# A transformer block with a mixture of experts on one core: the down product repacked to 128 rows, and the order around it

## What is computed

```python
xn = layernorm(x)                                  # (8, 256, 256)
q, k, v = xn @ Wq + bq, xn @ Wk + bk, xn @ Wv + bv # 16 heads of 16
q, k = rope(q), rope(k)
attn = softmax(causal(q @ k.T / 4)) @ v @ Wo + bo
scores = softmax(xn @ gate_w.T)                    # 64 experts, top 6 per token
routed = sum over the 6: w * (silu(g) * u) @ w_down[e].T   # g, u = xn @ w_gate_up[e].T, 176 wide each
shared = (silu(sg) * su) @ ws_down.T               # 2 shared experts of 176 (352 wide in all)
out = x + attn + routed + shared
```

## Time and profile before

| | us |
|---|---|
| three executions | 728.43, 731.99, 732.77 (median 731.99) |
| the profiled execution, its own time | 725.61 |
| its span, first to last instruction | 723.8 |
| busy in the span: PE, DVE, POOL, ACT | 674.7, 497.2, 396.6, 326.6 |
| mean granted TensorE clock | 0.981 of full speed |

### The profile page before, as it was taken

One profiled execution on the slowest core, in us unless ns is written; L12 is line 12 of the kernel. 1 busy time (PEld: TensorE's weight loads), 2 busy tenths in 40 slices (PEclk: granted clock), 3 DMA queues, 4 the chain that ended last, 5 costly groups with the idle time before them and its releaser, 6 DMA issues.

```text
span 723.8 us, 19510 instructions
## 1 busy us (share of the span) xinstructions
PE 674.7 (93%) x5200; PEld 434.2 (60%) x5202; DVE 497.2 (69%) x1184; ACT 326.6 (45%) x849; POOL 396.6 (55%) x383
## 2 busy tenths in 40 slices
PE   6899999989999999999999999999778998999996
PEld 3755677664555555555555555555456776677764
DVE  5498899856666666667666666656377779777751
ACT  2432322224444444444444444444446566656552
POOL 2000000227787777777787776763776776677520
PEclk9599999999999999999999999999989999999998
DMA  8500000037676766767676763342122312231310
GB/s 282 185 1 1 1 0 1 22 112 233 191 211 195 224 211 214 224 211 214 211 224 191 248 210 98 98 96 58 59 66 73 100 55 67 88 98 57 96 59 30
DMA packets 54288, 90.75 MB, mean 125 GB/s; under 512 B 8694, under 2 KB 32438, under 8 KB 54246
## 3 DMA queue, kind: packets, MB, share of 16 engines
q1 hardware_dynamic: 23494, 43.11, 19.9%
q0 software_dynamic: 10752, 29.37, 14.4%
q10 hardware_dynamic: 20000, 17.73, 7.3%
HBM read 69.21 MB, written 20.97 MB: 125 GB/s over the span
## 4 chain that ended last, share of the span: by engine, by line
PE 61%; DVE 9%; POOL 8%; DMA 7%; issue 6%; ACT 3%; DVEq 2%; SPq 2%; ACTq 1%; POOLq 0%
PE pair L1023 20%; PE pair L1058 10%; PE pair L933 6%; POOL wqkv_sb L436 5%; DMA lower<-wdn 5%; PE pair L1009 4%; PE bank L1032 3%; PE pair L1042 3%; PE bank L996 3%; DMA wqkv_sb<-y_rows,slot_i 3%; PE bank L1134 2%; DVE negm L829 2%; DVE space L806 2%; POOL space L432 2%; PE bank L1081 1%
## 5 line engine op out<-in xcount | busy, mean ns | idle before, releaser
L380 POOL DMA_INDIRECT lower<-xn_rows,idx_all x128 | 136.9, 1069 | 228.4 <-DVE idx_all L752 135.5
L1023 PE MATMUL pair<-space,work 128*64 (+1 forms) x768 | 166.0, 463 | 7.9 <-DMA lower<-wdn 3.3
L1058 PE MATMUL pair<-lower,work 88*64 x512 | 121.6, 379 | 1.3 <-ACT work L537 1.0
L1023 PEld LDWEIGHTS pair<-space,work 128*64 128x64 f32 x768 | 66.9, 136 | 80.3 <-issue 56.5
L522 ACT ACTIVATE work<-pair 128x176 f32<-128x176 f32 x160 | 51.5, 322 | 117.4 <-PE pair L1023 59.9
L1058 PEld LDWEIGHTS pair<-lower,work 88*64 88x64 f32 x512 | 69.6, 137 | 48.1 <-issue 11.2
L762 DVE TENSOR_TENSOR work<-work,pair 128x176 f32<-128x176 f32 x160 | 53.1, 333 | 60.5 <-ACT work L522 60.0
L812 DVE COPY space<-lower 88x512 f32 x64 | 78.8, 1231 | 22.2 <-issue 21.8
L1023 PE MATMUL pair<-wqkv_sb,work 128*64 128x352 f32 x256 | 89.4, 472 | 0.0
L529 ACT ACTIVATE lower<-pair 128x256 f32<-128x256 f32 x128 | 49.3, 385 | 77.7 <-PE pair L1058 77.7
L557 ACT ACTIVATE pT<-pair 128x768 f32<-128x768 f32 x64 | 52.0, 812 | 58.9 <-PE pair L1121 56.2
(11 more groups left out here) (171 smaller groups left out, 1346.9 us busy)
## 6 DMA issues: line engine op xcount, KB each, us to landing
space<-wgu SPq DMA_DIRECT2D x66, 352.0 KB
y_rows<-lower ACTq DMA_DIRECT2D x128, 128.0 KB
lower<-wdn SPq DMA_DIRECT2D x66, 176.0 KB
x_all<-x SPq DMA_DIRECT2D x4, 512.0 KB, 7.7
xn_rows<-qk_all SPq DMA_DIRECT2D x16, 128.0 KB, 2.0
lower<-xn_rows,idx_all POOLq DMA_INDIRECT x128
out<-x_all SPq DMA_DIRECT2D x8, 256.0 KB, 2.5
wqkv_sb<-wqkv SPq DMA_DIRECT2D x1, 768.0 KB, 12.5
```

The source lines that it names most:

```text
L380: po.indirect_dma_start(xg[:, r % XB, :], None, xn_rows[:, :], bass.IndirectOffsetOnAxis(idx_all[:, r:r + 1], 0)).then_inc(xg_in[r % XB], 16)
L1023: last = pe.matmul(pair[u % 2][strip, 0:2 * F], xgT[u][:, c, strip], n, start=c == 0, stop=c == EC - 1, skip_group_check=True)
L1058: last = pe.matmul(pair[u % 2][strip, 512:512 + E], hT[:, u % 2, c, strip], n, start=c == 0, stop=c == 1, skip_group_check=True)
```

## The change

**The down product.** The hidden features are laid out as 128 + 48 in place of 88 + 88. `hid` and `hT` hold two tiles in three blocks of 128: block 0 is tile 0's first 128 features, block 2 tile 1's, and block 1 the last 48 of tile 0 on rows 0 to 47 and the last 48 of tile 1 on rows 64 to 111. So two tiles take 3 transposes (`h_transpose` once a turn), one copy of 384 columns on ACT, and `down` for two tiles is 4 matmuls of 128 rows and then 4 of 48 rows, each of these in its own quarter of the array. The 48-row part of strip 0 reads `first_rest`, a new copy on DVE of 256 columns per tile (L849), because it must lie on the rows of its tile. The second product of `hidden` is two instructions (128 and 48 columns). `down` of both tiles waits for both copies of its turn (`rest_own`).

**Weights.** An expert is loaded by 5 DMAs in place of 2, the last 48 rows twice. POOL clears the unused rows of the ring in two pieces (`zeros_ok`).

**Registers.** PE's table `tile_s` holds the ring slot itself. PE no longer waits for weights (DVE's copy does). PE loads its registers between the 128-row and the 48-row matmuls. DVE loads two entries per tile, `own` and `first`, in place of one.

**Shared experts.** They run two tiles a turn, as the routed ones do, with 3 down matmuls of 128 rows for two steps (of one token tile, both experts) in place of 4 of 88. `LIST_AT` lists one token tile per turn.

**Attention.** The first nine scores alternate between `pair[0]` and `pair[1]`; the first two fills come before the last down product; `combine` comes before `normalise` in DVE's slot.

```diff
-LIST_AT = [3 * (t - LISTED_FIRST) // 2 - 1 for t in range(NT)]
+LIST_AT = [2 * (t - LISTED_FIRST) - (1 if t < 6 else 3) for t in range(NT)]
...
+                sp.dma_start(wdn_sb[0:FP, s, 0], dn[:, 0:E]).then_inc(w_loaded[s % 2], 16)
+                sp.dma_start(wdn_sb[FP:P, s, 0], dn[0:P - FP, E:2 * E]).then_inc(w_loaded[s % 2], 16)
+                sp.dma_start(wdn_sb[0:REST, s, 1], dn[P - FP:FP, E:2 * E]).then_inc(w_loaded[s % 2], 16)
+                sp.dma_start(wdn_sb[HALF:HALF + REST, s, 1], rest[P - FP:FP, E:2 * E]).then_inc(w_loaded[s % 2], 16)
...
             def hidden(i, u):
...
+                if k == 0:
+                    last = dve.tensor_tensor(hid[:, 0:F], sg[:, 0], up, ALU.mult)
+                else:
+                    dve.tensor_tensor(hid[:, 2 * P:3 * P], sg[:, 1, 0:P], up[:, 0:P], ALU.mult)
+                    last = dve.tensor_tensor(hid[:, P + HALF:P + HALF + REST], sg[:, 1, P:F], up[:, P:F], ALU.mult)
...
             def load_own(i, u):
                 dve.reg_load(own_reg[u], tile_e[0:1, 1, bass.ds(i, 1)])
+                dve.reg_load(first_reg[u], tile_e[0:1, 0, bass.ds(i, 1)])
...
+                e = dve.snap(first_reg[u], min_val=0, max_val=XT - 1) & (P - 1)
+                rows = slice(u % 2 * HALF, u % 2 * HALF + REST)
+                dve.tensor_copy(first_rest[rows], wdn_sb[rows, bass.ds((e + FIRST) % WB, 1), 1]
+                                .rearrange("p o n -> p (o n)")).then_inc(rest_own, 1)
...
-                wait_weights(pe, e)
...
+                pe.wait_ge(hT_ok, i + 2)
+                pe.wait_ge(rest_own, i - SHARED_TILES + 2)
...
+                for k in range(2):
+                    rows = slice(k * HALF, k * HALF + REST)
+                    for g, n in enumerate((first_rest[rows], own_dn[k][rows, 1])):
+                        strip = slice(g * GRAIN, (g + 1) * GRAIN)
+                        last = pe.matmul(pair[k][strip, 512:512 + E], h[rows, 1, strip], n, start=False, stop=True,
+                                         skip_group_check=True)
...
+        def scores_at(m):
+            return pair[m % 2 if m < AHEAD else 0][:]
```

More of the change, by code:

```diff
@@ L1027, in h_transpose @@
             def h_transpose(i, u):
[L1028 to L1034 removed]
+                o = bank[2 + u // 2]
+                pe.wait_ge(hid_ok, i + 2)
@@ L1064, in _ @@
[L1064 to L1070 removed]
+                for c, w in enumerate((wdn_sb[:, FIRST, 0], wdn_sb[:, FIRST, 1], wdn_sb[:, FIRST + 1, 0])):
+                    last = pe.matmul(pair[t % 2][:, 512:512 + E], hT[:, u // 2, c], w, start=c == 0, stop=c == 2)
```

230 lines of the change are left out of this document (136 added, 94 removed).

## The result

The changed kernel takes 776.93 us (median of six executions, 771.39 to 780.66); the kernel before, run beside it on the same chip, takes 732.34 us (728.43 to 734.2). The ratio is 1.061, with a 95% interval of 1.056 to 1.066: slower. The forecast was 729 us, and 776.93 lies outside its range. The profiled execution took 777.52 us with a span of 775.7 us and a mean granted clock of 0.944, where before it was 725.61, 723.8 and 0.981.

The account below looks back on a forecast made before the run. PE's work per turn was taken as the bound, DVE having 0.8 us of slack. Shared experts -5.5, weights +1, routed stage +6.7 and attention -5 gave -2.8 us, so 729 us on the median, range 715 to 743.

Parts of the forecast that it names:

- PE's turn, 4.83 us: Routed stage: PE's own work per turn falls from 5.28 to 4.83 us, with the 48-row products at 0.43.
- the guess of 0.1: PE's routed turn: 0.1 us added for changing the split of the array.
- The third rival: Routed down part: quarters run two by two, so it stays at 1.73 us; kernel 721 us; chance 0.12.
- DVE's turn, 5.50 us: Routed stage: DVE's sequencer becomes the bound at 5.40 to 5.64 us a turn, 5.50 taken; stage +6.7 us.
- My price of 0.41 us for a second load: DVE's routed turn: the added register load per tile costs 0.30 us plus 0.11 for its address step.
- The second rival: DVE's routed turn 6.0 us: loads at median or more (+0.48), POOL's blocking no longer hidden (+0.15); 760 us; chance 0.21.
- the third case: Slower case on whose side the prediction put the 600 ns load floor (turn 6.6 us, kernel some 64 us slower).
- Shared experts, -5.5: Shared stage: PE's shorter turns give -8.8 us, DVE's lateness +2, eight register loads +1.3; bounds -9 and 0.
- weights, +1: Between shared and routed stages: three more DMA issues per expert delay the first weights by 1 us; bounds 0 and +4.
- the 4.5: Shared stage: DVE's work per turn, 4.5 us, against PE's 3.99 and 0.35 for the listing.
- Attention, -5: Attention: two score buffers -2.2 us and `combine` ahead of `normalise` -2.8, sum -5; bounds -8.7 and +4.
- The ramp's -2.2: Start of attention: two score buffers shorten the distance between maxima from 2.45 to 1.7 us in three slots, -2.2 us.

Follow-up runs that it names:

- p0: The kernel before without POOL's rotary step, its biases and the output bias, gathers kept: 726.3 us, ratio to before 0.988 to 0.995.
- p3: Changed kernel without POOL's tensor work, one register load per tile on DVE, hidden copy first on ACT: 728.6 us, ratio to before 0.993 to 1.000.
- p1: Changed kernel without POOL's rotary step, its biases and the output bias, gathers kept: 751.6 us, ratio to before 1.020 to 1.034.
- p2: Changed kernel without POOL's tensor work and with one register load per tile on DVE: 742.2 us, ratio to before 1.009 to 1.020.
- a2: Changed kernel with one register load per tile on DVE in place of two: 771.6 us, ratio to before 1.036 to 1.057.
- a1: Changed kernel with `combine` put back behind `normalise`, `halves` and `residual` in DVE's attention slot: 765.4 us, ratio to before 1.035 to 1.051.
- a4: Changed kernel with down weights laid out by the host, two DMAs per expert in place of five: 784.5 us, ratio to before 1.048 to 1.066.
- c5: c4 with five DMAs per expert in place of two: 735.8 us, ratio to before 1.002 to 1.008.
- c4: c3 with the hidden copy ahead of the transposed x copies on ACT: 734.6 us, ratio to before 1.002 to 1.008.
- c3: Changed kernel with sums behind `normalise`, PE's late wait for the 48-row copies, one DVE load per tile, two DMAs per expert: 728.0 us, ratio 0.995 to 0.999.
- w1: Changed kernel with PE's wait for the 48-row copies (`rest_own`) moved behind the 128-row down products: 765.8 us, ratio to before 1.041 to 1.052.
- b1: The kernel before with `combine` ahead of `normalise`, `halves` and `residual` in DVE's attention slot: 744.9 us, ratio to before 1.013 to 1.024.
- a5: Changed kernel with PE's two register loads moved behind the 48-row products: 774.8 us, ratio to before 1.055 to 1.067.

## Why the prediction was wrong

**What bounds before.** PE's work per turn, with DVE 0.8 us in reserve. p0 fits: 4.2 us are all that POOL's tensor work cost there.

**PE's turn, 4.83 us.** Right as PE's own chain: 4.89 us in p3. Four 128-row pairs took 0.86 as forecast; the tails 0.59, up to the start of the transposes, for 0.43 and the guess of 0.1. The third rival is refuted, the quarters run together; the "pace of the array" by which attention's four products were read had no row behind it, so this was the first measurement. But in the changed kernel PE's turn is only reached when nothing waits, and a wait of 0.3 us ahead of the down part lengthens the part itself, to 1.97 us. The prediction had no such term.

**DVE's turn, 5.50 us: the step that failed.** It is the sentence "Contention does not come on top: the second down copy takes 1.26 us in the mean where the first took 0.42, blocked while POOL works, but the sequencer runs on behind it." With POOL at work the turn is 6.02 us, without its tensor work 5.66 (p1). The blocking is 0.37 us x 63 = 23 us of the changed kernel's stage, and 18.8 of the 37.4 that the change added. The sum without contention came near, 5.50 against 5.66, in part by luck: it has one value where p1's turns alternate between 5.2 and 6.0, and ACT's hidden copy is missing from it. The reasoning held before the change, when a blocked copy had its reserve to run out in. It failed because the down copies, the added one last, are what PE waits for, and because two copies stand behind each other on one engine, so a blocked one delays the next. That the sequencer goes on is of no use when the copy itself is waited for.

**The rest of the 37.4.** Without POOL's tensor work the changed kernel is still 0.30 us a turn over the old one (5.66 against 5.36), by DVE's sequencer and ACT's hidden copy in turn. p1, p2 and p3 take the covers off one by one: 5.66, 5.55, 5.33. My price of 0.41 us for a second load was too low for DVE itself: the two down copies of a turn start 1.67 us apart in the median of p1 (forecast 1.47) and 1.12 apart in p2, so the load costs DVE 0.55. But it was far too high for what it is worth to the kernel: 0.11 a turn in p2, where PE then waited for ACT, and 0.02 in the profile of a2. ACT I had called "still under PE's turn"; it was over it, since `hT_copy` stood behind `xgT_copy` and half of the up part.

**The second rival** named 6.0 us a turn, two loads at their median and blocking by POOL. The turn was 6.02, but by luck in the size: the place and the blocking were right, its price of 0.15 less than half of what it measured (0.37, or 0.30 more than in the old kernel), and the loads wrong (0.31 us in the median). Its sign, down copies that start more than 1.6 us apart, was met: 1.70 in the median of the changed kernel. Its 760 us missed through the other terms. The Trainium skill's floor of about 600 ns for a `tensor_load` (DMA: Bandwidth & Descriptors, section "Latency and other measured facts"), which the prediction tied to "the third case" and which points to this one, was not seen: the medians are 308 and 311 ns.

**Shared experts, -5.5, and weights, +1.** Right in size: from the first shared to the first routed up product it is 4.0 us less, for -4.5. The turn of 4.33 us, seen seven times, is the forecast's 3.99 and 0.35 for the listing, so there DVE needed less than the 4.5; in the three late turns it was late by more than the 0.16 forecast. The eight loads ahead of the first product were put at +1.3, and PE's wait there is 3.14 us. That the routed stage starts only 2.4 earlier is because the shared one began 1.6 later in this execution (0.3 in a1, with the same code ahead of it). Two DMAs per expert bring the start forward by 1.5 us in a4 and 1.7 between c5 and c4, near the +1. Of the 5.2 us by which c3 starts earlier (153.6), a2, a4 and w1 show 1.8, 1.5 and 1.0 alone.

**Attention, -5: wrong in sign.** `combine` ahead of `normalise` was put at -2.8, with a bound of +4 for rows that come late "in each of the sequences". It costs 15.1 us in a1 and 18.4 in b1. I had priced the waits that go, not what stands behind the instruction that would now wait: `normalise`, and behind it PE's projection, and behind that a clock that falls once per sequence (0.91 in attention; 0.98 in the profile before from 505 to 720 us, 0.93 in p0 and c3, where the sums also come last). The ramp's -2.2 did not show.

**The clock.** No term was given to it. In the routed stage it fell after waits of PE of 1.47, 1.89, 1.45 and 1.49 us, and added to each of them. After four others of that size (1.41 at 270.23, 1.81 at 339.89 and at 410.13, 1.55 at 486.21) it didn't, and what makes the difference stays open.

## What to carry to other kernels

Reserve that an engine has is reserve of a place in the order, not of a percentage: before you put a copy on an engine, ask who waits for that copy, and what the longest blocked copy of its kind takes (2.06 us here for a mean of 0.57 and a shortest of 0.28). Put a wait for late data behind the work that does not need it; w1 got 13.6 us in the stage by moving one line. And where four engines stand within 0.3 us of each other, an edit must be tried with the others around it: the same swap on ACT made p2 13.7 us faster, the changed kernel no faster and c3 6.6 us slower.

## What was not expected of the hardware

An idle PE can pay twice. In the changed kernel PE came 1.47 us late to a down part (PE's timeline):

```profile
216.17 0.42 PE L1128 MATMUL pair<-lower,work 128*64 x1 [1.47 <-DVE wqkv_sb L849]
...
217.48 0.44 PE L1137 MATMUL pair<-wqkv_sb,work 48*64 48x256 f32 x3 [0.23 <-issue]
...
219.97 0.85 PE L1070 MATMUL pair<-space,work 128*64 x1
...
222.99 0.38 PE L1128 MATMUL pair<-lower,work 128*64 x1
```

The granted clock from 217 to 222 us is 0.66, so it stood at its lower level of 1.2 GHz for most of it. From the first down product to the up part it took 3.80 us, and from there to the next down product 3.02; where the clock holds, the same distances are 2.88 (433.61 to 436.49) and at most 2.84 (to 439.33, with a wait of 0.32 in it). So 1.47 us of waiting cost 1.1 us more afterwards. Against the late turn at 374.52, behind which the clock stays at 1.00 (2.82 us to the up part at 377.34 and 2.51 to the next down product at 379.85), it is 1.5. Four such falls make some 4 to 6 us of the stage, an estimate from this one, and turns of 7.7 to 8.5 us in the profile of the changed kernel where a wait as long without a fall gives 6.8 to 7.2.

A 48-row DVE copy was held up beside POOL's gathers too, but little: in p1, up to 500 us, those that are held take 0.43 to 0.58 us, nearly all with nothing but a gather beside them. The 2.06 us come from a gather with a tensor operation right behind it: the copy waits for both. And PE's register loads cost nothing in the turns in which PE has not waited (0.86 us and no gap in p3), but show as a gap of 0.19 to 0.23 us between two groups of products when PE has waited; in a5, with the loads elsewhere, the gap is gone.
